# Maxima's scores ahead of each key tile's scores, and the split of the sums between the next unit's maxima, in a Trainium2 layer kernel

## The chip, the cores and the metric

The kernel runs on one core of a Trainium2 chip. A core has TensorE (matmuls, results in PSUM), VectorE, ScalarE and GpSimd (elementwise work and reductions), SyncE (DMA issue) and 16 DMA engines. They run side by side and are ordered by semaphores that the program sets. PSUM is read by VectorE and ScalarE; GpSimd works on SBUF. The metric is the device time of one execution in microseconds (us), the median of several runs.

## The reference

`x` is (4, 512, 128). It is normalised, and two branches read the result: attention with 16 heads of 64 and a LayerNorm behind it, and a mixture of 8 experts with the top 2 of each token.

```
xn = layernorm(x)
q, k, v = (xn @ Wq), (xn @ Wk), (xn @ Wv)        # 16 heads of 64
scores = einsum('bind,bjnd->bijn', q, k) / 8
probs = softmax(scores over keys)
attn = einsum('bijn,bjnd->bind', probs, v) @ Wo
A = gamma * norm(xn + attn) + beta
probs_e = top-2 of softmax(xn @ router_w.T), normalised
h = silu(xn @ gate_w[e] + gate_b[e]) * (xn @ up_w[e] + up_b[e])
F = sum_e probs_e * (h @ down_w[e] + down_b[e])
out = x + A + F
```

## The kernel before

The attention is worked off in 32 units: 4 sequences times 8 pairs of heads. A unit is 512 queries against 512 keys for two heads, in four key tiles of 128 (`kt`). The experts stand between units 29 and 30 (`HOST = 30`). Each engine has its own program, written out by hand, with its own order; nothing is scheduled automatically.

Every softmax needs a shift near its row's maximum before it is exponentiated. So for each unit `u + 1` TensorE computes, inside unit `u`, coarse scores (`scores_for_max`, L373, one pair of matmuls for each query tile `qt`) into PSUM banks 4 and 5 or 6 and 7 in turn. VectorE reduces each to its maxima (`maximum`, L866, into `q_top`). TensorE turns them (`turn_max`, L379, into bank 4), and VectorE writes the shift (`set_shift`, L871).

For its own unit TensorE does, for each key tile, three pairs of score matmuls (`scores`, L386; products of the high and low parts of q and k) and one pair that adds the shift (`scores_shift`, L392), then the coarse scores of round `kt` for the next unit. ScalarE exponentiates each key tile (`exponent`, L705, 128x1024). Score tiles alternate between two pairs of PSUM banks, so tile `kt` waits for the exponential of tile `kt - 2`. Behind the four tiles TensorE has a wait for the exponential of tile 2, and then `project(u + 2)` (L359, L360, L363: q and k of the unit after next), a part of v (L335 to L337), the output share of unit `u - 2` (L424), `turn_max`, `denominators(u - 1)` (L417, into bank 7) and `values(u - 1)` (L401, into bank 6).

The sums of the probabilities over the key tiles are made on GpSimd: `first_sums` (L1139, tiles 0 and 1, from the exponential of tile 1 on), then `other_sums` (L1147, tiles 2 and 3; and L1151 twice, one for each head), all of them SBUF to SBUF. In most units (all that are not in `WHOLE`) the sums are then split in two 16-bit parts for the matmul L417: ScalarE rounds them (L692), and VectorE makes the rest (`lower_sums`, L890, one instruction for each head, from `psums` and `sums_16`, both in SBUF). There are 23 such units, 4 to 9, 11 to 17, 19 to 25, 27, 28 and 30. `WHOLE` units use L411 on the unsplit sums.

VectorE's order in unit `u` is: `normalise(u - 2)` (L899, o_norm, needs the values of unit `u - 2`), four maxima, `lower` twice (L860, low parts of k and q), `set_shift`, `add_share` (L960), `invert` (L879) and `invert_more` (L884, `inv_den` and `guess`, both in SBUF), `lower_sums(u)`; then in some units `lower_xt` (L838), `keep_logits` (L850, L852), variances (L806 to L814), and in units 10, 18 and 26 the LayerNorm statistics of a finished sequence (L970 to L976). GpSimd has extra work behind its sums: the split of an expert's weights (L1173) in units 1 to 8, the routing tables up to unit 16, the scatter of tokens by indirect DMA (L1288) from unit 17 on, and four additions L1325 ahead of the experts.

Round 1 of the coarse scores writes banks 6 and 7, and so waits for `normalise` (`o_ready`); round 0 writes bank 4, which `set_shift` reads.

Of the kernel before, what the change touches and what calls it, by code (L numbers as in the profile page):

```python
# [5 lines left out]
ALU = mybir.AluOpType  # L6
# [18 lines left out]
TILES = 39  # L25
GROUPS = 10
ROW = D + 2
HOST = 30
# [4 lines left out]
UP = 4096.0  # L33


def layer_kernel(nc: bass.Bass, x, wq, wk, wv, wo, gamma, beta, router_w,
# [5 lines left out]
    with ExitStack() as ctx:  # L42
# [58 lines left out]
        psums = sb("psums", [P, 3, 2, S])  # L101
# [3 lines left out]
        sums_16 = sb("sums_16", [P, 2, 2, S], F16)  # L105
# [76 lines left out]
        xt_lo_ready = sem("xt_lo_ready")  # L182
# [107 lines left out]
        def splits(u):  # L290
            return sum(i not in WHOLE for i in range(u))
# [4 lines left out]
        def last(u):  # L296
            return u == UNITS - 1
# [19 lines left out]
        def _(pe):  # L317
# [47 lines left out]
            def scores_for_max(u, qt):  # L365
                par = u % 2
                if qt == 0:
                    pe.wait_ge(hi_ready, 2 * u + 2)
                if qt >= 2:
                    pe.wait_ge(top_ready, 4 * u + qt - 1)  # L370
                for h in range(2):
                    of = slice(DH * h, DH * h + DH)
                    mm = pe.matmul(psum[:, mx_bank(qt) + h, :], q_hi[of, par, P * qt:P * qt + P], k_hi[of, par, :],  # L373
                                   start=True, stop=True)
                mm.then_inc(top_scores, 1)
# [52 lines left out]
            def last_shares():  # L428
# [6 lines left out]
                for t in range(TB):  # L435
                    if t % 2 == 0:
                        pe.wait_ge(o_ready, LAST + 1 + t // 2)
                    pe.matmul(psum[:, t, 0:D], o_last[:, P * t:P * t + P], wo_sb[:, LAST % NP, :],
                              start=False, stop=True).then_inc(wo_ready, 1)

            def unit(u):
                more = u + 1 < UNITS
                for kt in range(TB):

                    if kt == 0:
                        pe.wait_ge(lo_ready, min(2 * u + 4, 2 * UNITS) if u else 2)
                        if u == 0:
                            pe.wait_ge(v_kept, len(FIRST))
                        if last(u):
                            pe.wait_ge(added, u - 2)  # L450
                    if kt == 1:
                        if u == 0:
                            pe.wait_ge(lo_ready, 4)
                        else:
                            pe.wait_ge(v_kept, slices_before(u))
                        if u == 1:
                            pe.wait_ge(rows_kept, 3)
                        if 3 <= u < HOST:
                            pe.wait_ge(added, u - 2)
                        if last(u):  # L460
                            pe.wait_ge(probs_ready, 4 * u)
                    if kt >= 2:
                        pe.wait_ge(probs_ready, 4 * u + kt - 1)
                    scores(u, kt)
                    if kt == 0:
                        pe.wait_ge(shift_ready, u + 1)
                    scores_shift(u, kt)
                    if more:
                        if kt == 0:
                            if 3 <= u <= 5:  # L470
                                pe.wait_ge(xt_lo_ready, u - 1)
                            if u == 2 or 6 <= u <= 8:
                                pe.wait_ge(logits_kept, u - 4 if u > 2 else 1)
                            if u == 14:
                                pe.wait_ge(counts_kept, 2)
                            if u == 19:
                                pe.wait_ge(table_kept, 1)
                        if kt == 1 and u >= 2:
                            pe.wait_ge(o_ready, u - 1)
                        if kt < 2 and u == HOST:  # L480
                            pe.wait_ge(y_kept, TILES - 1 + kt)
                        scores_for_max(u + 1, kt)
                pe.wait_ge(probs_ready, 4 * u + 3)
                if u + 2 < UNITS:
                    project(u + 2)
                if u + 2 < UNITS:
                    pe.wait_ge(probs_ready, 4 * u + 4)
                if u == 0:
                    pe.wait_ge(wv_split, 2)
                for n, (t, half, bank) in enumerate(slices(u)):  # L490
                    if n:
                        turn_rows()
                        turn_max(u + 1)
                    project_v(t, half, bank)
                if u >= 2:
                    output_share(u - 2, bank_of_share(u - 2))
                if more and u:
                    turn_max(u + 1)
                if u >= 1:
                    if last(u):  # L500
                        pe.wait_ge(o_ready, u - 1)
                    denominators(u - 1)
                if u == 1:
                    pe.wait_ge(rows_kept, 3)
                    route_logits(0, turn_bank)
                if 2 <= u <= 4:
                    turn(u - 1, turn_bank)
                if 5 <= u <= 7:
                    route_logits(u - 4, turn_bank)
                if u == 13:  # L510
                    count_slots()
                if u == 18:
                    sum_table()
                if u >= 1:
                    for kt in range(TB):
                        if u == HOST - 1 and kt == 2:
                            pe.wait_ge(added, HOST - 2)
                            turn_group(0)
                        values(u - 1, kt)
# [279 lines left out]
        def _(dve):  # L799
# [63 lines left out]
            def maximum(u, qt):  # L863
                dve.wait_ge(top_scores, 4 * u + qt + 1)
                tops = q_top[:, u % 2, :].rearrange("p (h t) -> p h t", h=2)
                dve.tensor_reduce(tops[:, :, qt], psum[:, mx_bank(qt):mx_bank(qt) + 2, :], AX.X, ALU.max)\  # L866
                   .then_inc(top_ready, 1)
# [16 lines left out]
                dve.scalar_tensor_tensor(out=inv_den[:, :], in0=inv_den[:, :], scalar=2.0, in1=guess[:, :],  # L884
                                         op0=ALU.subtract, op1=ALU.mult).then_inc(inv_ready, 1)

            def lower_sums(u):
                for h in range(2):
                    dve.wait_ge(sums_rounded, 2 * splits(u) + h + 1)
                    dve.scalar_tensor_tensor(out=sums_16[:, 1, h, :], in0=psums[:, u % 2, h, :], scalar=UP,  # L890
                                             in1=sums_16[:, 0, h, :], op0=ALU.mult, op1=ALU.subtract)\
                       .then_inc(sums_split, 1)

            def normalise(u):
                dve.wait_ge(pv_done, u + 1)
# [5 lines left out]
            def unit(u):  # L901
                more = u + 1 < UNITS
                if u >= 2:
                    normalise(u - 2)
                if u == HOST:
                    experts()
                if more:
                    for qt in range(TB):
                        maximum(u + 1, qt)
                if last(u):  # L910
                    for b in (3, 2, 1):
                        sum_y(b)
                if u + 2 < UNITS:
                    lower(u + 2, 1)
                    lower(u + 2, 0)
                if more:
                    set_shift(u + 1)
                if u == 0:
                    keep_router_rest()
                if u >= 2:  # L920
                    add_share(u - 2, bank_of_share(u - 2))
                if u >= 1:
                    invert(u - 1)
                    invert_more(u - 1)
                if u == HOST - 1:
                    keep_weights(0)
                    lower_group(0)
                if u not in WHOLE:
                    lower_sums(u)
                if 2 <= u <= 4:  # L930
                    lower_xt(u - 1, turn_bank)
                if u == 1:
                    keep_logits(0, turn_bank)
                if 5 <= u <= 7:
                    keep_logits(u - 4, turn_bank)
                if 1 <= u <= 3:
                    variances(u)
                if u in (10, 18, 26):
                    base_variances((u - 10) // 8)
                if u == 8:  # L940
                    dve.wait_ge(logits_kept, B)
                    dve.tensor_reduce(per_token[:, 0, :], prob[:, :, :], AX.X, ALU.max).then_inc(marked, 1)
                if 9 <= u <= 11:
                    dve.wait_ge(picked, u - 8)
                    dve.tensor_reduce(per_token[:, 1 if u == 10 else 3, :], routed[:, 3, :, :], AX.X, ALU.max)\
                       .then_inc(marked, 1)
                if u == 13:
                    dve.wait_ge(den_kept, 1)
                    dve.reciprocal(slot_cols[:, 0, :, 0], per_token[:, 2, :]).then_inc(weight_ready, 1)
# [576 lines left out]
```

## Time and profile before

| | before |
|---|---|
| median of 3 runs | 506.25 us (505.22 to 507.96) |
| profiled execution, its own time | 504.81 us |
| its span, first to last instruction | 502.8 us |
| TensorE busy | 486.4 us |
| VectorE busy | 415.5 us |
| GpSimd busy | 374.1 us |
| ScalarE busy | 306.2 us |

Times in the profile count from the first instruction. Shares of busy time are over the whole span; a matmul's end is modelled, so matmuls overlap in the rows.

### The profile page before, as it was taken

Reading aid. Unit: us, or ns where it says so; the run is one execution under the profiler, and the core shown is the slowest. Engines: PE = TensorE matmul, PEld = TensorE weight load, DVE = VectorE, ACT = ScalarE, POOL = GpSimd, SP = SyncE. Lnnn points to the kernel's source line nnn. Section 1 sums busy time; section 2 is a strip of 40 time slices with the busy share of each in tenths; the row PEclk is TensorE's granted clock in tenths of the full one; section 3 lists DMA queues with packets and bytes.
Section 4 is the critical chain, followed back from the end, with each engine's and each line's share of the span. In section 5 each row is a group of like instructions: output and inputs, shape, how many; then the busy total and the mean of one; then the engine's idle time right before and its main releaser. Section 6 shows DMA issues by size and latency. Waiting matters only on the chain.

```text
span 502.8 us, 8484 instructions
## 1 busy us (share of the span) xinstructions
PE 486.4 (97%) x3042; PEld 318.9 (63%) x3042; DVE 415.5 (83%) x652; ACT 306.2 (61%) x474; POOL 374.1 (74%) x322
## 2 busy tenths in 40 slices
PE   7999999999999999999999999999999999999983
PEld 5566555666666666666566666666665688888532
DVE  5888889988999898989988888888889666654797
ACT  2786677666675666666656666666566444444531
POOL 7898676666777685999988788788788655555780
PEclk9999999999999999999999999999999999999997
DMA  8910000000000003000000000000001222221511
GB/s 260 229 19 23 22 22 22 21 22 1 1 1 1 1 1 83 2 2 0 12 16 17 13 16 17 13 16 17 12 17 39 69 75 63 74 56 30 161 50 42
DMA packets 24796, 19.58 MB, mean 39 GB/s; under 512 B 2281, under 2 KB 22311, under 8 KB 24756
## 3 DMA queue, kind: packets, MB, share of 16 engines
q1 hardware_dynamic: 22484, 14.81, 11.6%
q0 software_dynamic: 2272, 4.24, 2.6%
q8 instruction: 25, 0.41, 0.3%
q14 instruction: 15, 0.12, 0.1%
HBM read 11.10 MB, written 8.40 MB: 39 GB/s over the span
## 4 chain that ended last, share of the span: by engine, by line
PE 80%; DVE 10%; POOL 4%; ACT 3%; issue 2%; DMA 1%; DVEq 0%; POOLq 0%; ACTq 0%
PE psum L386 16%; PE psum L401 16%; PE psum L373 5%; PE psum L392 5%; PE psum L424 4%; PE psum L359 4%; PE psum L575 3%; PE psum L363 3%; PE psum L360 3%; PE psum L417 2%; PE psum L552 2%; DVE q_top L866 2%; DVE inverse L884 2%; PE psum L554 2%; PE psum L553 2%
## 5 line engine op out<-in xcount | busy, mean ns | idle before, releaser
L705 ACT ACTIVATE probs<-psum 128x1024 f32<-128x1024 f32 x128 | 131.1, 1026 | 72.1 <-PE psum L392 65.7
L866 DVE TENSOR_REDUCE q_top<-psum 128x2 f32<-128x1024 f32 x128 | 151.2, 1222 | 7.4 <-PE psum L373 6.6
L1139 POOL TENSOR_TENSOR psums<-probs 128x1024 f32<-128x1024 f32 x32 | 76.7, 2396 | 56.7 <-ACT probs L705 55.8
L401 PE MATMUL psum<-probs,v_now 128*64 128x512 f32 x512 | 115.9, 594 | 0.0
L1151 POOL TENSOR_TENSOR psums<-psums 128x512 f32<-128x512 f32 x64 | 81.7, 1297 | 2.5
L1147 POOL TENSOR_TENSOR psums<-probs 128x1024 f32<-128x1024 f32 x32 | 76.7, 2396 | 1.2 <-ACT probs L705 0.9
L401 PEld LDWEIGHTS psum<-probs,v_now 128*64 128x64 f32 x512 | 35.4, 137 | 61.6 <-issue 58.1
L1295 POOL DMA_INDIRECT ys<-stage,home x39 | 38.1, 976 | 32.9 <-DVE stage L1091 20.7
L386 PE MATMUL psum<-q_hi,k_hi 64*128 64x512 f32 x256 | 56.3, 432 | 0.5 <-ACT probs L705 0.3
L373 PE MATMUL psum<-k_hi,q_hi 64*128 64x512 f32 x256 | 52.1, 399 | 0.9 <-DVE xt_lo L838 0.5
L386 PE MATMUL psum<-q_lo,k_hi 64*128 64x512 f32 x256 | 51.2, 392 | 0.0
L392 PE MATMUL psum<-shift,ones_r 64*128 64x512 f32 x256 | 51.2, 392 | 0.0
L386 PE MATMUL psum<-q_hi,k_lo 64*128 64x512 f32 x256 | 51.0, 391 | 0.0
L386 PEld LDWEIGHTS psum<-q_hi,k_hi 64*128 64x128 f32 x256 | 24.1, 183 | 35.4 <-issue 24.1
L1288 POOL DMA_INDIRECT xs_sorted<-xn,pos x32 | 34.8, 1088 | 8.3 <-issue 6.9
L698 ACT ACTIVATE inverse<-psum 128x512 f32<-128x512 f32 x32 | 19.1, 596 | 35.5 <-PE psum L417 22.0
L1082 DVE TENSOR_TENSOR hid<-psum,gated 128x256 f32<-128x256 f32 x39 | 16.5, 424 | 29.1 <-ACT gated L758 18.6
L879 DVE TENSOR_TENSOR inverse<-psum,inverse 128x512 f32<-128x512 f32 x32 | 22.1, 691 | 20.7 <-ACT inverse L700 20.7
L758 ACT ACTIVATE gated<-psum 128x256 f32<-128x256 f32 x39 | 14.9, 383 | 37.9 <-PE psum L556 37.9
L890 DVE SCALAR_TENSOR_TENSOR sums<-psums,sums 128x512 f16<-128x512 f32 x46 | 33.5, 766 | 0.2
L884 DVE SCALAR_TENSOR_TENSOR inverse<-inverse 128x512 f32<-128x512 f32 x32 | 32.5, 1016 | 1.1
L692 ACT ACTIVATE sums<-psums 128x512 f16<-128x512 f32 x46 | 28.3, 622 | 8.2 <-POOL psums L1151 8.2
(212 smaller groups left out, 970.3 us busy)
## 6 DMA issues: line engine op xcount, KB each, us to landing
xs_sorted<-psums SPq DMA_DIRECT2D x10, 260.0 KB, 7.0
xs_in<-xs_sorted SPq DMA_DIRECT2D x10, 260.0 KB, 2.9
y_in<-ys SPq DMA_DIRECT2D x8, 256.0 KB, 5.1
rest<-in_L_attn_h_dram SPq DMA_DIRECT2D x4, 256.0 KB, 5.2
stage<-in_L_ffn_gate_w_dram SPq DMA_DIRECT2D x8, 128.0 KB, 2.1
stage<-in_L_ffn_up_w_dram SPq DMA_DIRECT2D x8, 128.0 KB, 2.2
wd<-in_L_ffn_down_w_dram SPq DMA_DIRECT2D x2, 512.0 KB, 4.8
out_dram<-rest SPq DMA_DIRECT2D x3, 256.0 KB, 2.0
```

The costliest lines, as they stand in the source:

```text
L373: mm = pe.matmul(psum[:, mx_bank(qt) + h, :], q_hi[of, par, P * qt:P * qt + P], k_hi[of, par, :], start=True, stop=True)
L386: pe.matmul(psum[:, sc_bank + 2 * (kt % 2) + h, :], of_k[of, par, keys], of_q[of, par, :], start=(n == 0), stop=False)
L392: mm = pe.matmul(psum[:, sc_bank + 2 * (kt % 2) + h, :], ones_r[of, :], shift[of, u % 2, :], start=False, stop=True)
L401: mm = pe.matmul(o[DH * h:DH * h + DH, :], v_now[:, kt, at:at + DH], probs[:, par, kt, h, :], start=(kt == 0), stop=(kt == TB - 1))
L705: act.activation(probs[:, u % 2, kt, :, :], psum[:, bank:bank + 2, :], ACT.Exp, scale=SCALE)\
L866: dve.tensor_reduce(tops[:, :, qt], psum[:, mx_bank(qt):mx_bank(qt) + 2, :], AX.X, ALU.max)\
L884: dve.scalar_tensor_tensor(out=inv_den[:, :], in0=inv_den[:, :], scalar=2.0, in1=guess[:, :], op0=ALU.subtract, op1=ALU.mult).then_inc(inv ...
L1139: pool.tensor_tensor(psums[:, par, :, :], probs[:, par, 0, :, :], probs[:, par, 1, :, :], ALU.add)\
L1147: pool.tensor_tensor(psums[:, 2, :, :], probs[:, par, 2, :, :], probs[:, par, 3, :, :], ALU.add)\
L1151: pool.tensor_tensor(psums[:, par, h, :], psums[:, par, h, :], psums[:, 2, h, :], ALU.add)\
L1288: pool.indirect_dma_start(out=xs[:, :], out_offset=bass.IndirectOffsetOnAxis(ap=pos[:, slot, t:t + 1], axis=0), in_=xn[:, t, :], in_offset ...
L1295: pool.indirect_dma_start(out=ys[:, :], out_offset=bass.IndirectOffsetOnAxis(ap=home[:, i:i + 1], axis=0), in_=y_out[:, i % 4, :], in_offs ...
```

## The change

TensorE: for every unit from 2 on, the coarse scores of round `kt` for the next unit are issued ahead of the scores of key tile `kt`, with the waits that belong to them; the wait for the unit's own shift goes ahead of round 0 with them. Units 0 and 1 keep the old order. VectorE: `lower_sums` of unit `u` leaves the end of unit `u`. Its two halves are done in unit `u + 1`, one behind the maximum of round 2 and one behind that of round 3; in the last unit, which has no maxima, both come right behind `normalise`.

```
             def unit(u):
                 more = u + 1 < UNITS
+                ahead = u >= 2
                 for kt in range(TB):
+                    if ahead:
+                        if kt == 0:
+                            pe.wait_ge(shift_ready, u + 1)
+                        next_round(u, kt)
...
                     scores(u, kt)
                     if kt == 0:
                         pe.wait_ge(shift_ready, u + 1)
                     scores_shift(u, kt)
-                    if more:
...
-                        scores_for_max(u + 1, kt)
+                    if not ahead:
+                        next_round(u, kt)
```

`next_round(u, kt)` holds the waits and the call that stood there, unchanged:

```
+            def next_round(u, kt):
+                if u + 1 < UNITS:
+                    if kt == 0:
+                        if 3 <= u <= 5:
+                            pe.wait_ge(xt_lo_ready, u - 1)
+                        if u == 2 or 6 <= u <= 8:
+                            pe.wait_ge(logits_kept, u - 4 if u > 2 else 1)
+                        if u == 14:
+                            pe.wait_ge(counts_kept, 2)
+                        if u == 19:
+                            pe.wait_ge(table_kept, 1)
+                    if kt == 1 and u >= 2:
+                        pe.wait_ge(o_ready, u - 1)
+                    if kt < 2 and u == HOST:
+                        pe.wait_ge(y_kept, TILES - 1 + kt)
+                    scores_for_max(u + 1, kt)
```

On VectorE `lower_sums(u, h)` is now one half, called from `unit`:

```
                 if more:
                     for qt in range(TB):
                         maximum(u + 1, qt)
+                        if qt >= 2 and u and u - 1 not in WHOLE:
+                            lower_sums(u - 1, qt - 2)
+                if last(u) and u - 1 not in WHOLE:
+                    for h in range(2):
+                        lower_sums(u - 1, h)
...
-                if u not in WHOLE:
-                    lower_sums(u)
```

## Rows read from the trace of the kernel before

**Rows 1.** The page: busy time of each engine, share of the span, instructions.
```profile
PE 486.4 (97%) x3042; PEld 318.9 (63%) x3042; DVE 415.5 (83%) x652; ACT 306.2 (61%) x474; POOL 374.1 (74%) x322
```

**Rows 2.** Line L373: what its engine sat idle for, us and times.
```profile
  DVE o_norm L899: 2.1, 6
  DVE xt_lo L838: 1.4, 2
```

**Rows 3.** Timeline of unit 24, TensorE and ScalarE: start, us, what.
```profile
319.34 0.50 PE L386 MATMUL psum<-q_hi,k_hi 64*128 64x512 f32 x2
...
319.68 0.40 PE L386 MATMUL psum<-q_hi,k_lo 64*128 64x512 f32 x2
...
320.38 0.41 PE L373 MATMUL psum<-k_hi,q_hi 64*128 64x512 f32 x2
...
322.55 0.40 PE L392 MATMUL psum<-shift,ones_r 64*128 64x512 f32 x2
...
323.00 2.20 ACT L705 ACTIVATE probs<-psum 128x1024 f32<-128x1024 f32 x2 [0.23 <-PE psum L392]
...
324.29 0.50 PE L359 MATMUL psum<-xt_hi,wqk_hi 128*128 128x512 f32 x1
...
327.55 0.62 PE L417 MATMUL psum<-sums,parts 128*64 128x512 f16 x4
...
331.53 0.50 PE L386 MATMUL psum<-q_hi,k_hi 64*128 64x512 f32 x2
```

**Rows 4.** Waits of TensorE's weight loads: us in total, times, longest.
```profile
PEld psum L359 <- ACT probs L705: 10.8, 30, 0.4
```

**Rows 5.** Timeline of unit 24, VectorE.
```profile
319.88 0.68 DVE L899 TENSOR_TENSOR o_norm<-psum,inverse 128x512 f32<-128x512 f32 x1
320.82 4.81 DVE L866 TENSOR_REDUCE q_top<-psum 128x2 f32<-128x1024 f32 x4 [0.26 <-PE psum L373]
...
330.84 1.29 DVE L890 SCALAR_TENSOR_TENSOR sums<-psums,sums 128x512 f16<-128x512 f32 x2
```

**Rows 6.** Timeline of GpSimd: unit 24, and L1139 of unit 17.
```profile
322.85 2.40 POOL L1139 TENSOR_TENSOR psums<-probs 128x1024 f32<-128x1024 f32 x1 [1.90 <-ACT probs L705]
325.27 2.38 POOL L1147 TENSOR_TENSOR psums<-probs 128x1024 f32<-128x1024 f32 x1
327.73 2.51 POOL L1151 TENSOR_TENSOR psums<-psums 128x512 f32<-128x512 f32 x2
```
```profile
237.78 2.41 POOL L1139 TENSOR_TENSOR psums<-probs 128x1024 f32<-128x1024 f32 x1
```

**Rows 7.** Timeline of VectorE and GpSimd side by side, units 17 and 5.
```profile
242.59 3.02 POOL L1151 TENSOR_TENSOR psums<-psums 128x512 f32<-128x512 f32 x2
...
243.79 0.69 DVE L884 SCALAR_TENSOR_TENSOR inverse<-inverse 128x512 f32<-128x512 f32 x1
...
244.57 1.60 DVE L890 SCALAR_TENSOR_TENSOR sums<-psums,sums 128x512 f16<-128x512 f32 x1
```
```profile
92.55 1.29 POOL L1173 TENSOR_TENSOR w_lo<-stage,w_hi 128x512 fp32r<-128x512 f32 x1
92.55 1.83 DVE L884 SCALAR_TENSOR_TENSOR inverse<-inverse 128x512 f32<-128x512 f32 x1
```

**Rows 8.** Timeline of TensorE at the start of unit 5.
```profile
81.82 0.40 PE L392 MATMUL psum<-shift,ones_r 64*128 64x512 f32 x2
82.69 0.50 PE L373 MATMUL psum<-k_hi,q_hi 64*128 64x512 f32 x2 [0.47 <-DVE xt_lo L838]
```

**Rows 9.** Timeline of VectorE: units 10 and 11, and ahead of the experts.
```profile
148.25 4.60 DVE L866 TENSOR_REDUCE q_top<-psum 128x2 f32<-128x1024 f32 x4
...
158.05 0.86 DVE L970 BATCH_NORM_STATS2 stats<-acc 128x6 f32<-128x128 f32 x4
...
159.92 0.68 DVE L899 TENSOR_TENSOR o_norm<-psum,inverse 128x512 f32<-128x512 f32 x1
```
```profile
392.10 1.23 DVE L1075 COPY wcol<-xs_in 128x4 f32<-128x4 f32 x1
```

**Rows 10.** The page's costliest groups: busy us, mean ns of one, idle before.
```profile
L890 DVE SCALAR_TENSOR_TENSOR sums<-psums,sums 128x512 f16<-128x512 f32 x46 | 33.5, 766 | 0.2
```

More of the change, by code:

```diff
@@ L467, in unit @@
                     scores_shift(u, kt)
-                    if more:
[L469 to L481, printed above, removed]
-                        scores_for_max(u + 1, kt)
+                    if not ahead:
+                        next_round(u, kt)
                 pe.wait_ge(probs_ready, 4 * u + 3)
@@ L885, in invert_more, with lower_sums @@
                                          op0=ALU.subtract, op1=ALU.mult).then_inc(inv_ready, 1)
[L887 to L892, printed above, removed]
+            def lower_sums(u, h):
+                dve.wait_ge(sums_rounded, 2 * splits(u) + h + 1)
+                dve.scalar_tensor_tensor(out=sums_16[:, 1, h, :], in0=psums[:, u % 2, h, :], scalar=UP,
+                                         in1=sums_16[:, 0, h, :], op0=ALU.mult, op1=ALU.subtract)\
+                   .then_inc(sums_split, 1)
             def normalise(u):
```

## The prediction

> **What bounds the kernel now.** I read the page's engine totals first: TensorE is busy 97% of the span, VectorE 83% [rows 1]. With TensorE so full a gain must come from its waits, so next the waits of the moved instruction, the maxima's scores L373: 2.1 us for o_norm and 1.4 for xt_lo, together 3.5 us [rows 2]. That is about the most an earlier VectorE can give back at this line. Then the timeline of one ordinary unit, unit 24, engine by engine. It starts at 319.34 and the next at 331.53: 12.19 us [rows 3]. All times from here are offsets from the unit's start. A pair of matmuls (two heads side by side) takes one slot of 0.23 us, the first of a unit 0.34. The order is three slots of scores, one of shift, one of maxima's scores, four times over; then the projections L359 at +4.95, den's matmuls L417 at +8.21, and the values L401 from there to the unit's end, 3.98 after L417 [rows 3].
>
> TensorE has a small wait in the middle of every unit. L359's weight load waits for ScalarE's exponential of key tile 2, which runs from +3.66 to about +4.71 (half of the pair 2.20 long); L359 starts 0.24 after it [rows 3], and its load has waited 10.8 us for that in 30 units, 0.36 each [rows 4]. VectorE works from +0.54 (L899) to +12.7 with under 2 us of idle time, and L890, the split of the sums, is its last work of the unit: +11.50 to +12.79 [rows 5]. GpSimd adds from +3.51 to +10.90 without a gap: L1139 to +5.91, L1147 to about +8.35, L1151 twice [rows 6].
>
> **Part 1, TensorE's order (29 units, 2 to 30).** No matmul is added. The maxima's scores go from slot 5 of each round to slot 1, so each exponential's scores end one slot later. Key tile 2's shift L392 now begins at +3.21; it would begin at +3.44, the exponential would end at +4.94 and L359 start at +5.18. The maxima's fourth round no longer stands behind the last shift to cover that wait. So 0.23 us is lost in every unit, and nothing afterwards gives it back, as projections, shares, den and values are TensorE work in a row. Sum: 7 units without a split (2, 3, 4, 11, 19, 27, 30) x 0.23 = 1.6 us, and 0.23 in each other one. GpSimd's L1139, which waits for exponential 1, moves to +3.74 as well, and so ends at +6.14.
>
> **Part 2, the waits that move up.** The wait for o_norm stands ahead of round 1 of the maxima, now wanted at +1.27 (4 slots earlier). With the split gone from VectorE's end, L899 starts when the values end, about +0.1, and ends at +0.8: hidden. Of today's 3.5 us [rows 2] I let go what has L890 at its root: in unit 5 the first L373 comes 0.87 after L392 in place of 0.23, behind xt_lo [rows 8], 0.64; and of o_norm's 2.1 two waits of 0.4, in units 9 and 18. Together 1.4; the bounds are 0 and 3.5. In units 11, 19 and 27 VectorE has the LayerNorm statistics L970 to L976 ahead of L899, up to 1.9 us of them [rows 9]; see part 4. In units 2 to 4 it has the variances L806 to L814 there, a chain of the same kind, on a VectorE with more room: +0.5 us in all, between 0 and 3 x 0.6. The waits on xt_lo, logits and tables are otherwise met before their unit starts, or at the same instant; I take nothing for them. No DMA is issued by a moved step, and none waits on it.
>
> **Part 3, the split between the maxima (22 units: 46 L890 are 23 pairs, one of them goes to the last unit).** This decides. L890 reads two SBUF tensors (psums and sums_16). In the trace such a VectorE instruction does not run beside a GpSimd addition. Issued at 244.57 while the second L1151 was running (the two last from 242.59 to 245.61), the first of two L890 took 1.60 [rows 7], where a pair of them undisturbed takes 1.29 [rows 5] and the mean of all 46 is 0.77 [rows 10]. L884 at 92.55, issued with L1173 (92.55 to 93.84), took 1.83, and the one at 243.79 took 0.69 [rows 7]. Both long ones end 0.55 after GpSimd's instruction does: 246.17 against 245.61, and 94.38 against 93.84. In the other order GpSimd waits: the two L1151 that met L884 at 243.79 took 3.02 in place of 2.51, 0.5 more [rows 6, 7]. L866, which reads PSUM, shows no such thing: four in a row take 4.81 while L1139 runs [rows 5, 6], and 4.60 when VectorE has them back to back, 1.13 apart [rows 9].
>
> The Trainium skill, page "SBUF — State Buffer", section "Who interferes with whom", states it as a rule: a VectorE instruction with two SBUF inputs and a GpSimd instruction that reads SBUF exclude each other for a whole instruction, and the one that comes second waits. By that rule, the trace agrees (1.83 against 0.69). Without it the sum would be the first rival's below.
>
> Now VectorE's new walk. L899 at +0.1; maxima at +0.7, +1.83, +2.96; the first L890 is issued at +4.1. L1139 has run since +3.74 and ends at +6.14, so L890 ends at 6.14 + 0.55 = +6.7. L1147 begins at +6.14 by its row but gets going only 0.5 later: to 6.14 + 2.4 + 0.5 = +9.05. The fourth maximum runs from +6.6 to +7.8. The second L890 is issued at +7.75, inside L1147, and ends at 9.05 + 0.55 = +9.6. Den's matmuls L417 wait for both halves: with 0.05 to 0.1 for the semaphore, +9.65. Their own slot would be +8.44. So TensorE waits 1.2 us; behind L417 in its queue stand the 16 value matmuls, and they end the unit: 9.65 + 3.98 = +13.63, 1.44 us over 12.19 (0.23 of it from part 1).
>
> No 1024-element GpSimd addition is seen against a two-input VectorE operation in the trace. Bounds: none would wait, 0.23 a unit in all; both wait in full, 1.44. I take the latter, since the 512-element additions L1151 and L1173 do so in both cases shown, and L1139 and L1147 have the same form with twice the length. A semaphore or issue delay more or less gives 1.35 to 1.6.
>
> One unit is let off: in unit 17 L1139 starts late, since GpSimd still lays out the tables (237.78 [rows 6], +4.86 by the unit's start at 232.92; about +4.6 in the longer units); the first L890 slips in ahead of it and the second ends before +8.4: 0.23. So 21 x 1.44 = 30.2, plus 0.2.
>
> **Part 4, what VectorE has behind it.** From +9.5: L860 twice, L871, L960, L879 (0.6 to 0.7 each like L899, back to back) to +12.7, then L884 to +13.4, or +13.9 where GpSimd is in L1173 (units 5 to 8, which are 13.3 long today). The next L899 is wanted at +13.7. It just fits, so VectorE is nearly full but not yet the bound. Where L970 to L976 follow, it does not fit: L899 ends about 0.6 late for round 1 in units 11, 19 and 27, +1.8. Before the experts (unit 29) the copy L1075 meets one of GpSimd's additions L1325 already now and takes 1.23 [rows 9]; L884, later, will meet one too, which puts off xst_lo, for which the experts wait, by one addition more: +1.2. The last unit's split lies behind L899 and ahead of nothing urgent: 0.
>
> **Sum**: 30.2 + 0.2 + 1.6 + 0.5 + 1.8 + 1.2 - 1.4 = 34.1 us. The profiled execution took 504.81 (span 502.8), 1.44 below the median of the three runs; so 538.9 for it, and 506.25 + 34 = 540 for the median.
>
> **The rivals.**
> (a) The lock does not bite, because L890 is short or gets in between. Then the split ends by +6.7, before its need at +8.44, and only part 1 and the small terms are left: 29 x 0.23 + 0.5 - 1.4 = +5.8, 512 us. For it: most of the 46 ran undisturbed until now (mean 0.77 [rows 10]). Against: those met no addition of GpSimd; where they did they waited.
> (b) Faster: TensorE's new order costs nothing because the exponential of tile 2 is not what L359 really waits for, and an earlier VectorE takes away all waits of L373. 3.5 us less: 502.7. It is decided by L359's start: at +4.95 or before, this holds; and L417 must stay at or before +8.21. Against: the load waits on that exponential in 30 units [rows 4].
> (c) VectorE becomes the bound: its walk has 0.3 us to spare in a unit of 13.63. If one more instruction meets a GpSimd addition (L884 with the last L1151), L899 ends after +1.27 and round 1 of the maxima waits, near 0.6 in 21 units: +13, 553 us.
> (d) The two parts change nothing that can be measured, gains and losses of part 1 and 2 cancelling without the lock: 506.
>
> **How the numbers follow.** Forecast 0.82, (a) 0.08, (b) 0.03, (c) 0.05, (d) 0.02. A measurement of this kernel tells 0.5%, 2.5 us. Faster by more: (b), 0.03; within: (d), 0.03 with rounding; slower: 0.94. The forecast's own range is 21 units x 1.35 to 1.6 and the small terms half or double: 536 to 546. With room for an unseen term to either side, toward (a) and (c), 530 to 550 holds the time 8 in 10.
>
> **What the profile afterwards would show.** Part 1: L359 at +5.18, L373 ahead of L386. Part 3: L890's mean from 0.77 to about 2.2 us, with the first ending 0.55 behind L1139 and the second 0.55 behind L1147; L1147 at 2.9 in place of 2.4; L417 near +9.65 with a wait on L890, the ordinary unit 13.6 long. L373's wait for o_norm at units 11, 19, 27 alone. I am wrong if L890 keeps 0.68 among the maxima (then (a)), or if L417 starts before +9.

## The result, and the profile after

The changed kernel takes 538.72 us in the median of four runs (537.63 to 539.45); the kernel before, run beside it, takes 505.74 (503.11 to 507.96). The ratio is 1.0667, 95% interval 1.0627 to 1.0708. The profiled execution took 539.1 us with a span of 536.9, 34.1 more than the 502.8 before; the forecast was 540 and its sum was also 34.1. The granted clock was 0.994 of full speed in the mean over the span, as before (0.993), so the clock does not carry the difference; one stretch of 3.4 us at half speed (1.2 in place of 2.4 GHz) stands in unit 29 and is taken up there.

The page of the changed kernel: engine totals, shares of the chain of work that ended last, and the costliest groups that answer to [rows 1, 10].

```profile
PE 489.9 (91%) x3042; PEld 316.5 (59%) x3042; DVE 462.7 (86%) x652; ACT 301.8 (56%) x474; POOL 384.0 (72%) x322
...
DVE 37%; PE 34%; POOL 15%; issue 10%; ACT 2%; DMA 0%; DVEq 0%; POOLq 0%; ACTq 0%
...
L900 DVE SCALAR_TENSOR_TENSOR sums<-psums,sums 128x512 f16<-128x512 f32 x46 | 96.0, 2088 | 0.1
...
L1161 POOL TENSOR_TENSOR psums<-probs 128x1024 f32<-128x1024 f32 x32 | 85.6, 2674 | 1.4 <-DMA xs_sorted<-psums 1.4
...
L417 PE MATMUL psum<-sums,parts 128*64 128x512 f16 x92 | 14.4, 393 | 27.6 <-DVE sums L900 27.6
```

The same instructions are there (3042, 652, 474, 322). TensorE does the same work, but has 27.6 us of idle time ahead of the den's matmuls L417, all of it ended by the split, which is now L900. In the chain of work that ended last VectorE has the largest share, 37%, and GpSimd 15%. VectorE's busy time has grown by 47.2 us with no instruction added, and the split alone by 62.5 (33.5 to 96.0): what is busy in the record is waiting inside an instruction. All 46 instructions of the split, by line:

```profile
L900 DVE SCALAR_TENSOR_TENSOR sums<-psums,sums x46: 692/1720/2777, 87.1 to 511.9; 128x512 f16<-128x512 f32 x46
```

Minimum, median and maximum are 692, 1720 and 2777 ns; the mean was 766 [rows 10] and is 2088. The waits of TensorE on it and on the two others that the prediction speaks of:

```profile
PEld psum L417 <- DVE sums L900: 32.4, 22, 1.5
...
PE psum L417 <- DVE sums L900: 27.6, 22, 1.3
...
PEld psum L359 <- ACT probs L716: 11.7, 30, 0.4
```

22 waits, one for each pair ahead of which the den now stands: about 1.25 us each.

Unit 24 of the changed kernel, for [rows 3, 5, 6]. It starts at 343.83 and the next at 357.33: 13.50 us against 12.19. (L909 is o_norm, L877 the maximum, L900 the split, L1153, L1161 and L1165 GpSimd's additions; before they were L899, L866, L890, L1139, L1147 and L1151. L716 is the exponential, L705 before.)

```profile
343.83 0.50 PE L373 MATMUL psum<-k_hi,q_hi 64*128 64x512 f32 x2
...
348.43 0.40 PE L392 MATMUL psum<-shift,ones_r 64*128 64x512 f32 x2
348.77 0.50 PE L359 MATMUL psum<-xt_hi,wqk_hi 128*128 128x512 f32 x1
...
353.35 0.62 PE L417 MATMUL psum<-sums,parts 128*64 128x512 f16 x4 [1.24 <-DVE sums L900]
...
357.33 0.50 PE L373 MATMUL psum<-k_hi,q_hi 64*128 64x512 f32 x2
```
```profile
347.70 2.20 ACT L716 ACTIVATE probs<-psum 128x1024 f32<-128x1024 f32 x2 [0.21 <-PE psum L392]
```
```profile
343.96 0.69 DVE L909 TENSOR_TENSOR o_norm<-psum,inverse 128x512 f32<-128x512 f32 x1 [0.44 <-PE psum L401]
344.56 3.48 DVE L877 TENSOR_REDUCE q_top<-psum 128x2 f32<-128x1024 f32 x3
347.96 2.56 DVE L900 SCALAR_TENSOR_TENSOR sums<-psums,sums 128x512 f16<-128x512 f32 x1
350.44 1.21 DVE L877 TENSOR_REDUCE q_top<-psum 128x2 f32<-128x1024 f32 x1
351.58 1.72 DVE L900 SCALAR_TENSOR_TENSOR sums<-psums,sums 128x512 f16<-128x512 f32 x1
...
356.32 0.69 DVE L895 SCALAR_TENSOR_TENSOR inverse<-inverse 128x512 f32<-128x512 f32 x1
```
```profile
347.57 2.40 POOL L1153 TENSOR_TENSOR psums<-probs 128x1024 f32<-128x1024 f32 x1 [2.60 <-ACT probs L716]
349.98 2.77 POOL L1161 TENSOR_TENSOR psums<-probs 128x1024 f32<-128x1024 f32 x1
352.82 2.84 POOL L1165 TENSOR_TENSOR psums<-psums 128x512 f32<-128x512 f32 x2
```

Lay the last two blocks, VectorE's and GpSimd's, over each other. L1153 runs from 347.57 to 349.97. The first L900 begins at 347.96, inside it, and ends at 350.52, 0.55 after it. L1161 begins as L1153 ends and lasts 2.77, against 2.38 for the same addition before [rows 6]. The second L900 begins inside L1161 (to 352.75) and again ends 0.55 later, at 353.30; L417 starts 0.05 after that. One wait follows from the other: without the 1.88 that the first L900 loses, the second would be issued some 1.9 earlier, before L1161 begins.

By offsets from the unit's start, expected and found: first L900 issued +4.1, found +4.13; ended +6.7, +6.69; second ended +9.6, +9.47; L417 +9.65, +9.52; length 13.63, 13.50 (13.50 to 13.59 in units 20 to 26).

Unit by unit, the difference of the two profiled executions is this:

| units | predicted | found |
|---|---|---|
| 22 with a split among their maxima (5 to 29 without 11, 19, 27) | +30.2 | +29.6 |
| of these: unit 17 | +0.2 | +1.5 |
| of these: unit 29, with the experts | +2.6 | +2.5 |
| of these: units 5, 9, 18 beside an ordinary one | -1.4 | -1.4 |
| 2, 3, 4 | +1.2 | +2.2 |
| 11, 19, 27 | +2.5 | +1.5 |
| 30 | +0.2 | +1.0 |
| 0, 1, 31 and the start | 0 | -0.1 |

A unit starts here with its first matmul. That both columns add up to the same 34.1 is luck in part: rows missed by -0.6, +1.0, -1.0 and +0.8 cancel.

### The profile page after: what moved, and what is told of

The parts are those of the page before. It is cut to its first block, busy times and chain, and to the rows that moved or that the text cites. A ratio compares the mean times of both kernels' runs of the same rounds, so it can differ in the third digit from the quotient of the medians.

```text
span 536.9 us, 8503 instructions
## 1 busy us (share of the span) xinstructions
PE 489.9 (91%) x3042; PEld 316.5 (59%) x3042; DVE 462.7 (86%) x652; ACT 301.8 (56%) x474; POOL 384.0 (72%) x322
## 4 chain that ended last, share of the span: by engine, by line
DVE 37%; PE 34%; POOL 15%; issue 10%; ACT 2%; DMA 0%; DVEq 0%; POOLq 0%; ACTq 0%
DVE q_top L877 14%; DVE sums L900 12%; PE psum L401 11%; POOL psums L1161 4%; POOL psums L1165 4%; POOL psums L1153 4%; PE psum L586 3%; PE psum L386 3%; DVE o_norm L909 3%; PE psum L563 2%; PE psum L417 2%; PE psum L564 2%; PE psum L565 2%; PE psum L567 2%; DVE inverse L895 2%
## 5 line engine op out<-in xcount | busy, mean ns | idle before, releaser
L716 ACT ACTIVATE probs<-psum 128x1024 f32<-128x1024 f32 x128 | 131.1, 1027 | 88.3 <-PE psum L392 72.7
L877 DVE TENSOR_REDUCE q_top<-psum 128x2 f32<-128x1024 f32 x128 | 149.8, 1215 | 3.6 <-PE psum L373 3.4
L1153 POOL TENSOR_TENSOR psums<-probs 128x1024 f32<-128x1024 f32 x32 | 76.7, 2396 | 79.8 <-ACT probs L716 76.7
L401 PE MATMUL psum<-probs,v_now 128*64 128x512 f32 x512 | 117.6, 601 | 0.0
L900 DVE SCALAR_TENSOR_TENSOR sums<-psums,sums 128x512 f16<-128x512 f32 x46 | 96.0, 2088 | 0.1
L1165 POOL TENSOR_TENSOR psums<-psums 128x512 f32<-128x512 f32 x64 | 89.4, 1417 | 2.5
L1161 POOL TENSOR_TENSOR psums<-probs 128x1024 f32<-128x1024 f32 x32 | 85.6, 2674 | 1.4 <-DMA xs_sorted<-psums 1.4
L401 PEld LDWEIGHTS psum<-probs,v_now 128*64 128x64 f32 x512 | 35.7, 138 | 62.2 <-issue 58.8
L373 PE MATMUL psum<-k_hi,q_hi 64*128 64x512 f32 x256 | 54.8, 424 | 2.7 <-DVE o_norm L909 2.5
L386 PE MATMUL psum<-q_hi,k_hi 64*128 64x512 f32 x256 | 53.1, 409 | 1.8 <-ACT probs L716 1.7
L373 PEld LDWEIGHTS psum<-k_hi,q_hi 64*128 64x128 f32 x256 | 24.1, 184 | 34.5 <-issue 23.3
L417 PE MATMUL psum<-sums,parts 128*64 128x512 f16 x92 | 14.4, 393 | 27.6 <-DVE sums L900 27.6
L1302 POOL DMA_INDIRECT xs_sorted<-xn,pos x32 | 31.6, 988 | 8.3 <-issue 7.0
L424 PEld LDWEIGHTS psum<-wo_sb,o_norm 128*128 128x128 f32 x240 | 31.2, 191 | 3.2 <-ACT probs L716 1.0
```

The lines of the kernel that those rows point to most:

```text
L386: pe.matmul(psum[:, sc_bank + 2 * (kt % 2) + h, :], of_k[of, par, keys], of_q[of, par, :], start=(n == 0), stop=False)
L401: mm = pe.matmul(o[DH * h:DH * h + DH, :], v_now[:, kt, at:at + DH], probs[:, par, kt, h, :], start=(kt == 0), stop=(kt == TB - 1))
L716: act.activation(probs[:, u % 2, kt, :, :], psum[:, bank:bank + 2, :], ACT.Exp, scale=SCALE)\
L1153: pool.tensor_tensor(psums[:, par, :, :], probs[:, par, 0, :, :], probs[:, par, 1, :, :], ALU.add)\
L1161: pool.tensor_tensor(psums[:, 2, :, :], probs[:, par, 2, :, :], probs[:, par, 3, :, :], ALU.add)\
L1165: pool.tensor_tensor(psums[:, par, h, :], psums[:, par, h, :], psums[:, 2, h, :], ALU.add)\
```

## The experiments

The theories that the runs were to part were the prediction's own (the split meets GpSimd's additions), against these: that TensorE's new order is what costs; that the split is in the wrong place whether or not GpSimd is at work; and, for the small wait at L359, that it is not the exponential's. Lines are those of each kernel; where a number differs from the changed kernel's, the operation says which it is.

**The new order alone.** TensorE's order as changed, the split back at the end of VectorE's unit:

```
                         maximum(u + 1, qt)
-                        if qt >= 2 and u and u - 1 not in WHOLE:
-                            lower_sums(u - 1, qt - 2)
...
+                if u not in WHOLE:
+                    for h in range(2):
+                        lower_sums(u, h)
```

> TensorE's new order alone; the split of the sums stays at the end of VectorE's unit. Theory 1 (the record's part 1, each L359 0.23 us later): ordinary units (20 to 28) 12.42 us in place of 12.19, and L899, still behind the split, comes too late for the earlier round 1 in the units where VectorE has extra work, about 7 us in all: 506 + 6.7 + 7 = 519 us. Theory 2 (L359 is held by the change from 64-row to 128-row matmuls, not by the exponential, so the order is free): ordinary units stay at 12.19, only the late L899 costs: 512 us. Rival, the order is what made the kernel slow: over 530.

Measured: 521.27 us (518.99 to 522.87), ratio 1.0299 (1.0248 to 1.0349). That is more than either expectation, but not by the way of L417, which stands at +8.31 and waits for nothing. What is late is o_norm. Unit 9 of this kernel:

```profile
140.86 2.36 DVE L900 SCALAR_TENSOR_TENSOR sums<-psums,sums 128x512 f16<-128x512 f32 x2
...
143.34 0.67 DVE L909 TENSOR_TENSOR o_norm<-psum,inverse 128x512 f32<-128x512 f32 x1
```
```profile
140.35 1.72 POOL L1184 TENSOR_TENSOR w_lo<-stage,w_hi 128x512 fp32r<-128x512 f32 x1
```
```profile
142.51 0.40 PE L392 MATMUL psum<-shift,ones_r 64*128 64x512 f32 x2
...
144.07 0.50 PE L373 MATMUL psum<-k_hi,q_hi 64*128 64x512 f32 x2 [1.16 <-DVE o_norm L909]
```

The split of the old unit runs into the new one (from 141.47 on) and meets what GpSimd does behind its sums, the split of an expert's weights (L1184, to 142.07; 2.36 for two in place of 1.29 [rows 5]). L909 ends at 144.01, and the maxima's scores, wanted at 142.74, start at 144.07. In this kernel's ordinary unit L909 ends at +1.29 against a need at +1.27, which costs 0.1; in units 4 to 7, 9 to 13 and 15 to 18 the unit is longer by 0.2 to 2.4 (in unit 5 most of the 1.9 is not the order's: from 86.1 to 89.5 the granted clock is half, and the slots are 0.43 us in place of 0.23). So the new order has a price of its own when the split stays at the end, 15 us by the medians, and moving the split takes that price away and puts its own in its place.

**The split alone.** The changed kernel with `ahead = False`, so that TensorE keeps its old order.

> The split of the sums behind maxima 2 and 3 alone; TensorE keeps its old order. Theory (the two halves wait for GpSimd's L1139 and L1147 and hold up L417): L417 at +9.4 in place of +8.2, ordinary unit 13.4, about 534 us. Rival (the order is what costs): below 510.

Measured: 531.34 us (529.78 to 533.86), ratio 1.0503 (1.0463 to 1.0542). VectorE and GpSimd, and the den's matmuls:

```profile
346.25 2.41 POOL L1153 TENSOR_TENSOR psums<-probs 128x1024 f32<-128x1024 f32 x1 [2.36 <-ACT probs L716]
347.76 1.44 DVE L900 SCALAR_TENSOR_TENSOR sums<-psums,sums 128x512 f16<-128x512 f32 x1
348.66 2.77 POOL L1161 TENSOR_TENSOR psums<-probs 128x1024 f32<-128x1024 f32 x1
350.26 1.72 DVE L900 SCALAR_TENSOR_TENSOR sums<-psums,sums 128x512 f16<-128x512 f32 x1
...
352.03 0.62 PE L417 MATMUL psum<-sums,parts 128*64 128x512 f16 x4 [1.04 <-DVE sums L900]
```

Both halves wait here too, and the ordinary unit is 13.27 us long, with L417 at +9.28. The whole chain lies 0.23 earlier than in the changed kernel because GpSimd's first addition starts at +3.50 and not at +3.74. The first half is issued later into L1153 and so waits less (1.44 against 2.56), but it ends 0.54 behind it all the same: between the two places tried, 0.4 and 1.5 us into the addition, it makes no difference when the split is issued.

**The split without its second read of SBUF.** The changed kernel, with the first operand of L900 taken from the PSUM bank that was just reduced instead of from psums; it is multiplied by 0, so the low parts of the sums come out as zeros and are left out of the den. Place, size and semaphores stay.

```
-                            lower_sums(u - 1, qt - 2)
+                            lower_sums(u - 1, qt - 2, mx_bank(qt))
```

> The changed kernel, with the moved instruction reading its first operand from PSUM (the bank just reduced) in place of psums, same shape, and writing zeros: the low parts of the sums are left out. It then has one SBUF operand. Theory (two SBUF operands against a GpSimd addition exclude each other): it takes 0.68 each time, L417 back at +8.2, L1147 back at 2.4 us; 507 us, or 513 if part 1 of the record (0.23 a unit) holds. Rival (the place in the order costs, not the ports): stays near 538.

Measured: 508.97 us (508.71 to 512.96), ratio 1.0081 (1.0042 to 1.0120).

```profile
325.10 2.40 POOL L1157 TENSOR_TENSOR psums<-probs 128x1024 f32<-128x1024 f32 x1 [1.61 <-ACT probs L716]
325.47 0.68 DVE L904 SCALAR_TENSOR_TENSOR sums<-psum,sums 128x512 f16<-128x512 f32 x1
327.20 0.68 DVE L904 SCALAR_TENSOR_TENSOR sums<-psum,sums 128x512 f16<-128x512 f32 x1
327.49 2.38 POOL L1165 TENSOR_TENSOR psums<-probs 128x1024 f32<-128x1024 f32 x1
329.57 0.62 PE L417 MATMUL psum<-sums,parts 128*64 128x512 f16 x4
```

The first half runs inside the addition in 0.68 us, the second addition is back at 2.38 (2.77 with the lock), L417 stands at +8.22 without a wait, and the unit is 12.21 long. This one operand carries the wait: same place, same engine, same length of work. The run also takes away the read of psums, whose other half GpSimd is writing meanwhile, but the wait does not need that: L884, which reads inv_den and guess, waited in the same way in [rows 7]. The run also shows the price of the new order by itself where nothing is late: in 19 of the 22 split units the difference to before is between -0.4 and +0.2. Units 2 to 4 (+2.2), 10 (+0.6), 11 (+1.3) and 30 (+1.1) add up to 5.2; the span is only 4.3 longer, mainly because the first unit begins 1.3 earlier.

**One instruction for both halves.** 128x1024 behind maximum 2, with the semaphore raised by 2.

```
+                dve.scalar_tensor_tensor(out=sums_16[:, 1, :, :], in0=psums[:, u % 2, :, :], scalar=UP,
...
-                        if qt >= 2 and u and u - 1 not in WHOLE:
-                            lower_sums(u - 1, qt - 2)
+                        if qt == 2 and u and u - 1 not in WHOLE:
+                            lower_both(u - 1)
```

> The changed kernel with both halves of the split as one instruction of 1024 elements behind maximum 2. Theory (a whole-instruction lock, first come first served): it waits once, for L1139, ends near +7.25, the fourth maximum near +8.35, L379 and L417 about 0.4 late: ordinary unit 12.6, about 517 us. Rival (the two engines share bandwidth, so the cost goes by elements): near 538 as before.

Measured: 521.4 us (520.53 to 521.91), ratio 1.0313 (1.0276 to 1.0350). The ordinary unit is as expected, the time 4 us above it; units 10 and 11 are longer than before by 1.7 each.

```profile
334.58 2.40 POOL L1159 TENSOR_TENSOR psums<-probs 128x1024 f32<-128x1024 f32 x1 [1.13 <-ACT probs L716]
334.95 3.12 DVE L900 SCALAR_TENSOR_TENSOR sums<-psums,sums 128x1024 f16<-128x1024 f32 x1
336.99 3.29 POOL L1167 TENSOR_TENSOR psums<-probs 128x1024 f32<-128x1024 f32 x1
337.99 1.21 DVE L877 TENSOR_REDUCE q_top<-psum 128x2 f32<-128x1024 f32 x1
...
339.25 0.33 PE L379 MATMUL psum<-ident,q_top 128*128 128x128 f32 x1 [0.22 <-DVE q_top L877]
339.51 0.62 PE L417 MATMUL psum<-sums,parts 128*64 128x512 f16 x4
```

It waits once and not twice, and the second wait is gone; the unit is 12.67 long in place of 13.50. L417 stands at +8.68, no longer held by the split but by L379 ahead of it, which waits for the fourth maximum. GpSimd in turn is held 0.9 longer (3.29), in place of 0.4. So of the 1.31 that the changed kernel loses in an ordinary unit, about 0.8 is the second wait.

**Both halves among the early maxima.** The changed kernel, with the halves behind maxima 0 and 1 (`if qt < 2`), before GpSimd's first addition starts.

> The changed kernel with the halves of the split behind maxima 0 and 1. They would start near +1.9 and +3.6, both before L1139 (+3.74). Theory (lock, first come first served): no wait for VectorE, L1139 some 0.5 longer and that hidden, ordinary unit 12.2; units 2 to 4 keep their late L899 (about +2), the old late ones go: 506 us, 504 to 508. Rival (the second half just misses and waits for L1139): ordinary unit over 12.5, 515 us.

Measured: 513.53 us (512.91 to 515.29), ratio 1.0125 (1.0081 to 1.0169): between the expectations, and a miss for what I thought likely. Unit 24 and unit 10:

```profile
328.39 0.68 DVE L900 SCALAR_TENSOR_TENSOR sums<-psums,sums 128x512 f16<-128x512 f32 x1
...
330.12 0.68 DVE L900 SCALAR_TENSOR_TENSOR sums<-psums,sums 128x512 f16<-128x512 f32 x1
330.29 2.78 POOL L1153 TENSOR_TENSOR psums<-probs 128x1024 f32<-128x1024 f32 x1 [1.39 <-ACT probs L716]
```
```profile
152.84 2.38 POOL L1153 TENSOR_TENSOR psums<-probs 128x1024 f32<-128x1024 f32 x1 [3.55 <-ACT probs L716]
152.99 2.78 DVE L900 SCALAR_TENSOR_TENSOR sums<-psums,sums 128x512 f16<-128x512 f32 x1
```

The split now takes its 0.68 and GpSimd is the one that waits, 0.4 of an addition. The ordinary unit is 0.15 longer than before. But in unit 10, where the half comes 0.15 after the addition has begun, it takes 2.78: the loser is whoever is issued second, and 0.3 us decides. Of the 9.7 us by which the profiled span is longer than before, units 10 and 12 alone cost 3.2, and units 2 to 4 another 2.3.

**Both halves behind the last maximum.** One run.

> The changed kernel with both halves of the split behind maximum 3. The first is issued near +5.25 inside L1139 and ends near +6.7. Theory 1 (first come first served): L1147, waiting since +6.14, goes before the second half, which ends near +9.6; L417 at +9.5 as in the changed kernel, 538 us. Theory 2 (VectorE, back to back, keeps its turn): the second half ends near +7.3, L417 at +8.2, 508 us.

Measured: 544.32 us, span 542.2. The span is 5.4 us longer than the changed kernel's. Its first unit begins 4.8 us later and unit 6 has 1.7 of its own (both under the last heading), while unit 2 is some 0.8 shorter; the rest stands where the changed kernel does: ordinary unit 13.51, L417 at +9.52.

```profile
353.23 2.40 POOL L1153 TENSOR_TENSOR psums<-probs 128x1024 f32<-128x1024 f32 x1 [2.60 <-ACT probs L716]
354.74 4.21 DVE L900 SCALAR_TENSOR_TENSOR sums<-psums,sums 128x512 f16<-128x512 f32 x2
355.64 2.77 POOL L1161 TENSOR_TENSOR psums<-probs 128x1024 f32<-128x1024 f32 x1
...
359.01 0.62 PE L417 MATMUL psum<-sums,parts 128*64 128x512 f16 x4 [1.23 <-DVE sums L900]
```

Two halves back to back take 4.21 us in place of 1.29. The first waits for L1153; the second, issued at once behind it, waits again, because L1161 was already standing in line. Turns are taken one instruction at a time, so putting the halves together does not make them pass together; only one instruction does (above).

**The split right behind o_norm.** TensorE's old order, both halves behind `normalise(u - 2)`, ahead of the first maximum: away from GpSimd's additions, with room of up to +3.5.

> TensorE's old order; both halves of the split behind L899 and ahead of the maxima. L899 starts with the end of the values, the maxima at +1.9 in place of +1.5, back to back, the fourth ends near +6.5 as now. Theory: the o_norm waits of units 5, 9 and 18 go, nothing is added: 504.3 us, 503 to 505.5. Rival (a later start of the maxima delays L379 or L860): 506 to 510.

Measured: 507.3 us (504.38 to 510.69; 12 runs), ratio 1.0001 (0.9959 to 1.0042). No difference, where 504.3 was expected. By units, -0.7 in unit 5 and -0.4 in unit 18, where the late waits of [rows 2, 8] are gone, against +0.5 in unit 10, +0.1 in 15 and +0.1 in 29, where the first maximum is put off; in unit 9 the wait stays. The split can be had free here, but no gain from moving it is shown. One of up to 1 us is not excluded: the six runs with a granted clock of 0.993 or more have a median of 504.9, the 16 of the kernel before with 0.992 or more 505.9.

**What L359 waits for.** The kernel before, with the exponential of key tile 2 over one head of the two in units 2 to 29 (the other head's probabilities of that tile are left stale):

```
+                n = 1 if kt == 2 and 2 <= u < HOST else 2
+                act.activation(probs[:, u % 2, kt, 0:n, :], psum[:, bank:bank + n, :], ACT.Exp, scale=SCALE)\
```

> The kernel before, with the exponential of key tile 2 done for the first of the two heads only, from unit 2 to 29 (the other head's part of that tile is left out). It ends 0.5 us earlier. Theory 1 (the record: L359 waits for it): L359 at +4.82, ordinary unit 12.07, 502.5 us. Theory 2 (the 0.36 us between the last 64-row pair and the first 128-row matmul is a change of mode): L359 stays at +4.95, unit 12.19, time the same, 505.7.

Measured: 505.66 us (504.49 to 511.2), ratio 0.9981 (0.9946 to 1.0017); unit 12.18, L359 still at +4.93. Its wait, to be held against [rows 4]:

```profile
PEld psum L359 <- issue: 10.1, 28, 0.4
```

The exponential ends 0.4 us sooner, the wait is as long as before (10.1 us in the 28 units with the short exponential, 10.8 in 30), and no other engine stands behind it any more. It is not ScalarE's.

## Why the prediction was right, and where its steps were not

**The lock (part 3)**, that such a split and a GpSimd addition exclude each other, held, and nearly all of its numbers with it: both halves end 0.55 behind the addition that they meet, L417 waits about 1.25 (1.2 said), and 1024-element additions lock out as the 512-element ones did in [rows 7]. The two assumptions that were only bounded, that the long additions behave so and that both halves wait, are shown by the changed kernel and by the runs with no second read (1.0081), early halves (1.0125) and one instruction (1.0313). That the Trainium skill, page "SBUF — State Buffer", section "Who interferes with whom", says a VectorE instruction with at most one SBUF input, outside the 2-port performance modes, does not contend with GpSimd is what the run with the PSUM operand shows (0.68 against 2.56). An ordinary unit lost 1.31 in place of 1.44: L1161 is lengthened by 0.39, not 0.5, which I had taken from a pair of L1151, so the second half ends 0.13 sooner than the sum had it.

**The order's 0.23 a unit (part 1)** was wrong in its mechanism. I had L359 wait for the exponential and go to +5.18. It stayed at +4.94, though the exponential ended at about +4.9 instead of +4.7. From the last pair of 64-row matmuls to the first 128-row one it is 0.34 to 0.36 us in both kernels (348.43 to 348.77 above; 323.93 to 324.29 before), where pairs of one kind stand 0.23 apart:

```profile
323.93 0.43 PE L373 MATMUL psum<-k_hi,q_hi 64*128 64x512 f32 x2
```

In the changed kernel the exponential ends only 0.05 ahead of L359 (half of the pair that begins at 347.70, then L359 at 348.77), so this kernel cannot tell the two apart; the run on the kernel before does, where the exponential is shortened and the wait does not shrink. The Trainium skill, page "TensorEngine Tiling (Array Packing)", section "Key Properties", says that a change of tiling mode drains TensorE; a step of 0.11 to 0.13 us at the change from 64 to 128 rows agrees with it, though no run here takes the change of mode away. The releaser that the trace names was the last semaphore, not the cause. The 0.23 came back by another way: GpSimd's first addition starts 0.23 later, as said, and in split units all that follows hangs on it. That is the difference between 13.27 with the old order and 13.50 with the new. So the number held in these units although its reason did not, which is luck.

**The waits that move up (part 2).** The wait for xt_lo is gone from unit 5 and those for o_norm from 9 and 18, worth 1.4, as said. In units 2, 3 and 4 the new order cost 2.2 together where I had 0.5 + 0.7: o_norm comes behind the variances and starts at +1.57 in unit 2, +1.24 in 3 and +0.91 in 4, and the maxima's scores wait for it. In unit 2 one of the variances' instructions (L825, at 42.54) takes 0.85 in place of the 0.17 before, and ends with GpSimd's split of weights (42.09 to 43.37); in the two runs with the new order where it falls behind that instruction (one instruction, and behind the last maximum) it takes 0.17 and unit 2 loses 0.5 in place of 1.3. In 11, 19 and 27 it cost 1.5 where I had 2.5; 0.7 of the difference is that L359 was not late on top. The waits of L373 on o_norm by the page's count:

```profile
  DVE o_norm L909: 8.0, 12
```

8.0 us against 2.1 [rows 2]. Both count matmuls and weight loads together, so the prediction's 3.5 counts waits twice: before, the matmuls themselves sat idle 0.4 us for o_norm and 0.5 for xt_lo, the weight loads 1.7 and 0.9. Rival (b)'s 3.5 us of gain rests on it.

**Unit 17 (0.2 said, 1.5 found).** I let it off because GpSimd is late there. But in the longer units the tables are ready sooner by the unit's own clock: L1153 starts at +3.94, before L900 at +4.12, which then waits 2.78. The step that failed is "+4.6".

**Unit 29** lost 2.5 (2.6 said), but not by the steps said. L884 took 1.22 us there before, ending behind the last L1151, and takes 1.12 now, behind the first of the four additions: the 1.2 us of part 4 did not come. Two other things did. L417 stands at +9.57 like elsewhere, but before the change it stood at +7.51 there and not at +8.2, so it comes 2.1 later. And the granted clock is half for 3.4 us, while the values are worked on:

```profile
421.44 3.52 PE L401 MATMUL psum<-probs,v_now 128*64 128x512 f32 x8
```
```profile
421.30:424.70 3.40, 3.40 (x12) 0.73 (x8) 3.37 (x6) 1.23 (x2) 3.40 (x4) 0.50 0.00 0
```

The second row is a stretch with the busy times of TensorE, its weight loads, VectorE, ScalarE and GpSimd, then the granted clock, 0.50. In the run of the split alone the same eight matmuls take 1.88 at full clock, and the unit lost 1.8. With 0.23 for the order that makes 2.0, so the clock's part is some 0.4, an estimate. That 2.5 met 2.6 is luck.

**Unit 30** lost 1.0 (0.2 said), but this is not the change's: it is longer than before by 1.0 to 1.7 in all of the eight experiments' profiles, also in the one that only shortens an exponential (+1.7 there). The profile before looks like the exception. In the changed kernel, at 502.4, ScalarE and VectorE go on together, 2 us after their matmuls' start; what holds them is open.

**The parts do not add up by themselves.** Order alone +15, split alone +25, together +33 and not +40: the split's move relieves o_norm, which is what makes the order costly.

Rivals: (a), no lock, is what the run with the PSUM operand makes true by hand, and it gave 509 where the rival said 512: its 0.23 a unit is not there, and units 2 to 4, 10, 11 and 30 cost more than it had. (b) had L359 right, at +4.94, and L417 wrong. (c) did not come: VectorE's walk ends at +13.2 with L895, and o_norm still starts at +0.13. (d), no change, is out by 33 us. Part 4 calls units 5 to 8 13.3 long; units 5 and 8 were 14.0 and 12.2, but no term rests on it.

## What to carry to other kernels

Before an instruction of VectorE with two SBUF operands is moved, look at what GpSimd runs at its new place: issued inside an addition of 2.4 us, a 0.68 us instruction took up to 2.8 here, and the next one waited for the next addition. If it must be there, take one operand from PSUM where the data allow it, or make one instruction of two, or issue it clear ahead of the addition; and see whether GpSimd's start wanders by more than the margin. When a wait's releaser is named, check that the wait moves with it before a sum is built on it.

## What was not expected of the hardware

- Two VectorE instructions back to back give way in between to a GpSimd instruction that already waits (4.21 us for both). What GpSimd loses to a VectorE instruction that goes first is about 0.4 us at 512 elements (2.77 against 2.38) and 0.9 at 1024 (3.29), in place of the 0.68 and more that the instruction itself lasts.
- The first unit starts 18.8 to 20.1 us after the span's start in six of the ten profiles and 24.2 to 24.7 us in four (the split alone, behind o_norm, half exponential, behind the last maximum), though all kernels begin alike. In these four TensorE waits 2.9 us for one tile of xn (L321), where the other six wait 1.0 at most, and around that wait the granted clock falls to half for 3.4 or 6.8 us. Why xn is late is open. Single times of one kernel fall into two groups as well: of the 23 of the kernel before, 16 took 504.0 to 506.9 us with a mean granted clock of 0.992 to 0.998, and 7 took 507.7 to 510.9 with 0.988 to 0.990. So near no change the units' lengths tell more than the spans.
- One unit of two profiles is longer by 1.7 us than its neighbours of the same kind: unit 7 of the split alone, and unit 6 with both halves behind the last maximum. In both the granted clock is half for 3.4 us (125.7 to 129.1 and 113.5 to 116.9), and the 16 value matmuls L401 take 5.35 us in place of 3.65. Ahead of it TensorE had waited 1.0 and 1.2 us for the split and run eight small matmuls; in unit 6 of the changed kernel it did the same and the clock stayed. Why it fell is open.
